# An adaLN transformer block: the order of ScalarE's first square roots, identity products on TensorE, and the place of the row modulation

## The reference, cut to what matters

```
mod = (silu(c) @ wmod).reshape(4, 6, 1, 256)
sa, ca, ga, sb, cb, gb = (mod[:, n] for n in range(6))
ga, gb = (2 * (g >= 0) - 1) * maximum(abs(g), 0.25)      # for both gates
h = layernorm(x) * (1 + ca) + sa                          # x is (4, 1024, 256)
x = x + ga * attention(h)                                 # 16 heads of 16
h = layernorm(x) * (1 + cb) + sb
x = x + gb * (mixture of 32 experts, 6 of them per token, and a shared expert)(h)
```

## Time and profile before

| | |
|---|---|
| time, median of 3 runs | 1390.08 us (1389.21 to 1391.02) |
| the profiled execution | 1387.17 us |
| its span | 1385.1 us |
| TensorE busy | 1329.3 us, 96% |
| VectorE busy | 1118.9 us, 81% |
| ScalarE busy | 737.3 us, 53% |
| GpSimd busy | 650.8 us, 47% |

### The profile page before, as it was taken

The page is one execution under the profiler, slowest core; times in us unless marked ns, Lnnn a source line. Parts: engine busy times, 40 slices in busy tenths (PEclk is TensorE's granted clock), DMA queues, the critical chain, the costliest instruction groups (busy, mean ns, idle before and its releaser), DMA issues.

```text
span 1385.1 us, 30718 instructions
## 1 busy us (share of the span) xinstructions
PE 1329.3 (96%) x8199; PEld 661.3 (48%) x8200; DVE 1118.9 (81%) x2809; ACT 737.3 (53%) x1127; POOL 650.8 (47%) x941
## 2 busy tenths in 40 slices
PE   6999999999999999999999999999999999999895
PEld 4562223323323223233232333577788888888542
DVE  6879999999999999999999983755566666666498
ACT  3551777767776777677776776123333333343100
POOL 1300123425745746557456467357655555555200
PEclk9996899999999999999999999999999999999998
DMA  6678655436356355463554437767666656665698
GB/s 208 225 232 199 136 159 104 93 78 151 67 139 149 97 116 113 120 166 64 130 145 148 116 112 236 229 195 230 219 201 200 204 176 186 178 176 177 254 340 328
DMA packets 264906, 235.31 MB, mean 170 GB/s; under 512 B 159286, under 2 KB 230470, under 8 KB 264684
## 3 DMA queue, kind: packets, MB, share of 16 engines
q1 hardware_dynamic: 237452, 159.23, 44.5%
q0 software_dynamic: 21872, 68.07, 13.7%
q10 hardware_dynamic: 5488, 6.82, 1.5%
HBM read 129.78 MB, written 104.22 MB: 169 GB/s over the span
## 4 chain that ended last, share of the span: by engine, by line
PE 70%; DVE 13%; DMA 4%; issue 2%; ACT 1%; POOL 1%; SPq 0%; DVEq 0%; ACTq 0%; POOLq 0%
PE psO L1274 15%; PE psE L1261 14%; PE ex_psGU L1787 12%; PE psM L1251 10%; DVE piece_max L1150 8%; PE ex_psY L1802 6%; PE ex_psX L1776 3%; PE psM L582 2%; DMA wide<-results 2%; PE ex_psA L1796 2%; PE co_psS L2056 2%; DMA results<-vals_inv,places 1%; ACT wide L1215 1%; PE late_psGU L2036 1%; PE late_psX L2047 1%
## 5 line engine op out<-in xcount | busy, mean ns | idle before, releaser
L1150 DVE TENSOR_REDUCE piece_max<-psM 128x1 f32<-128x512 f32 x1024 | 642.1, 681 | 19.4 <-PE psM L1251 15.8
L1215 ACT ACTIVATE wide<-psE 128x1024 f32<-128x1024 f32 x512 | 496.9, 1021 | 199.2 <-PE psE L1261 196.1
L1251 PE MATMUL psM<-wide 48*128 48x512 bf16 x1024 | 322.9, 394 | 9.3 <-DVE piece_max L1150 7.2
L1261 PE MATMUL psE<-wide 49*128 49x512 bf16 (+1 forms) x2048 | 328.9, 380 | 3.0 <-ACT wide L1215 2.8
L1868 POOL DMA_INDIRECT results<-vals_inv,places x223 | 213.9, 959 | 152.7 <-DVE vals_inv L1854 88.2
L1274 PE MATMUL psO<-wide 128*32 128x512 f32 x2048 | 273.6, 606 | 0.6 <-ACT wide L1215 0.6
L1251 PEld LDWEIGHTS psM<-wide 48*128 48x128 bf16 x1024 | 78.0, 93 | 334.0 <-DVE piece_max L1150 277.3
L1787 PE MATMUL ex_psGU<-wide,ex_xT 128*128 x892 | 231.1, 382 | 0.7 <-ACT ex_xT L1819 0.7
L1261 PEld LDWEIGHTS psE<-wide 49*128 49x128 bf16 (+1 forms) x2048 | 117.2, 95 | 94.2 <-ACT wide L1215 13.7
L1787 PEld LDWEIGHTS ex_psGU<-wide,ex_xT 128*128 128x128 f32 x892 | 152.1, 190 | 14.9 <-issue 2.7
L1819 ACT ACTIVATE ex_xT<-ex_psX 128x256 f32<-128x256 f32 x223 | 85.4, 383 | 123.3 <-PE ex_psX L1776 121.5
(11 more groups left out here) (285 smaller groups left out, 1248.1 us busy)
## 6 DMA issues: line engine op xcount, KB each, us to landing
wide<-qk_parts SPq DMA_DIRECT2D x384, 64.0 KB
wide<-results SPq DMA_DIRECT2D x16, 1536.0 KB, 9.4
rows<-lists SPq DMA_DIRECT2D x112, 160.0 KB
h2Ts<-lists SPq DMA_DIRECT2D x111, 160.0 KB
qk_parts<-parts SPq DMA_DIRECT2D x32, 384.0 KB, 2.9
xin<-in_x_dram SPq DMA_DIRECT2D x16, 512.0 KB, 4.1
wide<-in_guT_dram SPq DMA_DIRECT2D x3, 2560.0 KB, 13.6
lists<-pad_row SPq DMA_DIRECT2D x32, 160.0 KB
```

The source lines that it names most:

```text
L1150: v.tensor_reduce(piece_max[:, qh, (x * PAIRS + h) * KT // QH + qt, kh:kh + 1], bank_of("piece", PIECES * group + n), AX.X, ALU.max, negat ...
L1215: nc.scalar.activation(probs[:, step % 2, 2 * pair:2 * pair + 2], psE[:, pair], ACT.Exp, scale=HD ** -0.5).then_inc(exp_ok, 1)
L1251: nc.tensor.matmul(bank_of(*user), qa[g][rows, h, qt * P:(qt + 1) * P], ka[g][rows, h, kh * 512:(kh + 1) * 512], start=True, stop=True).th ...
L1261: mm = nc.tensor.matmul(psE[:, pair, x], k[g][part, pair, kt * P:(kt + 1) * P], q[g][part, pair, qh * 512:(qh + 1) * 512], start=(q is qa) ...
```

## The change

Three things. On ScalarE `modulate(0, k)` stands ahead of `deviation(1)`. On TensorE 12, 4 and 5 products of the identity with itself (`keep_clock`, 128 columns, into a part of `psV` that nobody reads) stand ahead of `modulation()`, behind it, and behind `turn(0)`. And the row modulation moves from chunk 1, where it came after the keys, into the last chunk, where there is no next chunk to turn or modulate: it takes the place of `turn` on TensorE and of `modulate` on ScalarE, with its result in `psT`. Its two loops are exchanged.

```
--- before.py
+++ after.py
@@ -156,7 +156,7 @@
     NARROW = 2 * D
     WIDE = 4 * D
     SHARE = 5
-    ROWS_AT = 1
+    WARM = (12, 4, 5)
     with ExitStack() as ctx:
         def sb(name, shape, dt):
             return ctx.enter_context(nc.sbuf_tensor(name, shape, dt))
@@ -441,15 +441,17 @@
             def rows_modulation():
                 act.wait_ge(rows_done, 1)
                 for n in range(4):
-                    nc.scalar.activation(mod_rows[row_of[n]], psV[row_of[n], 1, 0], ACT.Copy).then_inc(rows_ok, 1)
+                    nc.scalar.activation(mod_rows[row_of[n]], psT[row_of[n], 0, 0:D], ACT.Copy).then_inc(rows_ok, 1)
 
             def chunk(c):
                 first(c, 0)
                 second(c, 0)
                 first(c, 1)
-                for k in range(KC):
-                    if c + 1 < NCH:
+                if c + 1 < NCH:
+                    for k in range(KC):
                         modulate(c + 1, k)
+                else:
+                    rows_modulation()
                 second(c, 1)
                 if c + 2 < NCH:
                     deviation(c + 2)
@@ -457,16 +459,14 @@
                 first(c, 3)
                 second(c, 2)
                 second(c, 3)
-                if c == ROWS_AT:
-                    rows_modulation()
 
             act.dma_start(wmod_c[:], wmod[:, :, 0:NARROW]).then_inc(wmod_c_in, 16)
             act.wait_ge(c_in, 16)
             nc.scalar.activation(scT[:], cT[:], ACT.Silu).then_inc(silu, 1)
             deviation(0)
-            deviation(1)
             for k in range(KC):
                 modulate(0, k)
+            deviation(1)
             for c in range(NCH):
                 chunk(c)
 
@@ -480,6 +480,10 @@
                         mm = nc.tensor.transpose(psT[:, k, i * P:(i + 1) * P], xhat[:, c % 2, i, k * P:(k + 1) * P],
                                                  env.ident[:])
                     mm.then_inc(turned, 1)
+
+            def keep_clock(n):
+                for _ in range(n):
+                    nc.tensor.matmul(psV[:, 0, 0, 0:P], env.ident[:], env.ident[:], start=True, stop=True)
 
             def queries_keys(c, j):
                 if j == 0:
@@ -506,17 +510,15 @@
 
             def rows_modulation():
                 pe.wait_ge(wmod_r_in, 16)
-                pe.wait_ge(v_ok, 2 * ROWS_AT)
-                for n in range(4):
-                    for k in range(KC):
-                        last = nc.tensor.matmul(psV[row_of[n], 1, 0], scT[:, k], wmod_r[:, k, n * D:(n + 1) * D],
+                pe.wait_ge(modulated, KC * NCH)
+                for k in range(KC):
+                    for n in range(4):
+                        last = nc.tensor.matmul(psT[row_of[n], 0, 0:D], scT[:, k], wmod_r[:, k, n * D:(n + 1) * D],
                                                 start=(k == 0), stop=(k == KC - 1))
                 last.then_inc(rows_done, 1)
 
             def values(c):
                 for n in range(2):
-                    if c == ROWS_AT and n == 1:
-                        pe.wait_ge(rows_ok, 4)
                     wait(pe, v_ok, 2 * (c - 1) + n + 1)
                     for i in range(2):
                         for k in range(KC):
@@ -524,19 +526,22 @@
                                                   env.wqkv[:, 2, k, :], start=(k == 0), stop=(k == KC - 1))
                     mm.then_inc(v_done, 1)
 
+            pe.wait_ge(zero, 2)
+            keep_clock(WARM[0])
             modulation()
-            pe.wait_ge(zero, 2)
+            keep_clock(WARM[1])
             turn(0)
+            keep_clock(WARM[2])
             pe.wait_ge(chan_ok, 2)
             for c in range(NCH):
                 queries_keys(c, 0)
                 queries_keys(c, 1)
                 if c + 1 < NCH:
                     turn(c + 1)
+                else:
+                    rows_modulation()
                 queries_keys(c, 2)
                 queries_keys(c, 3)
-                if c == ROWS_AT:
-                    rows_modulation()
                 values(c)
```

## The result

The changed kernel takes 1394.73 us in the median of 11 runs (1391.37 to 1398.74), the kernel before 1390.08 in 11 runs on the same chip. The ratio is 1.0032, with a 95% interval of 1.0021 to 1.0043: 2.9 to 6.0 us slower. The forecast was 1392.6 in a range of 1388.0 to 1396.0.

The account below looks back on a forecast made before the run. VectorE was taken to set the pace in the projection phase's steady chunks, with a five-engine barrier behind it. GpSimd's late last arrival (+2.3) and a slow first attention product (+0.2) gave +2.5 us: 1392.6, range 1388.0 to 1396.0.

Parts of the forecast that it names:

- The front: Start of the projection phase: TensorE's first products at 13.5 rather than 16.54, VectorE's first split at 18.85, 1.94 us sooner.
- VectorE sets the pace: Steady chunks: normalisations 11.25 us apart set the time; TensorE by itself can gain no more than 0.8 us.
- My sum over VectorE: Projection phase: VectorE reaches its last normalisation 5.16 us sooner; with 0.6 of slack TensorE reaches the last chunk 5.76 sooner.
- The bearing of a failed clock: Start: products beginning at 15.5, two of them slow, still give the whole 1.94 us at VectorE's first split.
- rival B: Start: identity products stay slow and in the way, first products at 17.2, +5.9 us, 1396.0; chance 0.09.
- GpSimd's tail: Last chunk: GpSimd's row work loses its cover, lands at 113.0 less 0.4, so the last arrival is +2.3 us.
- my reduction by 0.4: GpSimd's row work in the last chunk: taken 0.4 us shorter than in chunk 1, from a range of nothing to 0.8.
- rival A: End of the projection phase: GpSimd's row work is hidden, phase ends with VectorE at -4.7 us, 1385.4; chance 0.09.
- Rival C: Attention phase: low clock reaches further, 1.5 to 2.5 us more, 1394.1 to 1395.1; chance 0.12, with a GpSimd DMA drain.
- the -4.7 that I had for the other engines: End of the projection phase: TensorE, VectorE and ScalarE finish 4.7 us sooner, from -5.76 and +1.07.

Follow-up runs that it names:

- e5: The changed kernel measured again without alteration, on another chip; ratio 1.0022 to the kernel before, boundary 113.38.
- e6: The changed kernel without the 21 identity products; ratio 1.0042 to the kernel before, boundary 114.11.
- e10: The changed kernel with GpSimd's row work behind the barrier and without the identity products; ratio 0.9967 to the kernel before, boundary 107.75.
- e9: The changed kernel with GpSimd's row work behind the barrier, measured a second time; ratio 0.9972 to the kernel before, boundary 106.42.
- e4: The changed kernel plus 36 identity products on TensorE behind the last values; ratio 1.0029. Its mark is VectorE's second transposed row of maxima.
- e3: The changed kernel with GpSimd's nine row operations, four DMAs and their wait moved behind the barrier; ratio 0.9977, median 1385.59 against 1389.2 us.
- e8: The changed kernel with only GpSimd's wait for the four DMA landings moved behind the barrier; ratio 1.0043 to the kernel before, boundary 113.33.

## Why the prediction was right, and where a size was off

**The front.** The numbers are right, and close: products at 13.39 for 13.5, VectorE's first split at 18.94 for 18.85, its normalisations at 27.60, then 11.26 us apart until 83.89, which is 5.03 us sooner than before (forecast 5.16). TensorE 5.62 sooner at the last chunk (5.76).

The reason that I gave for them, that in the steady chunks "VectorE sets the pace", holds for one profile only, the changed kernel's first. There TensorE has 67.55 us between chunk 1 and the last chunk, 0.4 more than its own 67.17. In every other profile, e5 of the same kernel too, TensorE runs through these chunks without a wait for VectorE, 11.20 us a chunk; VectorE takes 11.26, and TensorE's lag of 0.8 us is not used up within eight chunks. So what comes sooner at the last chunk is what TensorE's own chunk 1 begins sooner (3.7 us here, 3.3 in e5) and the 2.3 us less in chunk 1. My sum over VectorE gave 3.26 for the first (TensorE's 0.6 included) and 2.50 for the second. That the two ways come within 0.3 us of each other is luck, and this part of the forecast owes its size to it.

**The bearing of a failed clock.** The prediction says that "products that start at 15.5, two of them slow, still give all of it". That is right for VectorE's first split and wrong for the end of the phase. In e6 the split does not wait, and yet the 0.75 us that TensorE begins chunk 1 later are 0.73 at the boundary; in e10 against e9 it is 1.33 for 1.33. It was no idle question. The granted clock stayed up in the changed kernel's first profile only. In e9, which is one of seven later profiles with identity products, all with a turn of 1.97 us, it was down before the turn:

```profile
8.74 2.05 PE L490 MATMUL psV<-ident 128*128 128x128 f32 x8
11.12 1.97 PE L484 MATMUL psT<-ident,xhat 128*128 128x128 f32 x8 [0.32 <-DVE xhat L339]
12.88 2.17 PE L490 MATMUL psV<-ident 128*128 128x128 f32 x10
14.89 3.60 PE L499 MATMUL psQK<-hT,wqkv 128*128 128x512 f32 x8
```

The five behind the turn then end at 15.0 and not at 13.3, where the chunk is ready at 13.9: for a slow clock they stand in the way by 1 us. In e9 the clock is back for the wide products (3.60 us for eight passes), so rival B (products at 17.2) did not occur, and VectorE's split is at 18.67 even so.

**GpSimd's tail.** The step on which the sign rested, and it was right: copies at 97.77 for 97.7, GpSimd at 99.52 for 99.43. Its sizes were off in three places that nearly cancel. The nine operations and the issues took 11.4 us from the first to the last issue's start, the same 11.44 as in chunk 1, so my reduction by 0.4 was wrong: L262 did come down (1.07 and 1.10), but L260 took 1.21 and L263 1.07 once each, beside VectorE, and the first issue took 0.79 again, with VectorE idle. The landings took 1.6 to 1.8 and not 2.1; the last was at 112.5. And the barrier opened 0.8 after it, not the 0.4 that it takes behind SyncE's last issue. Together +2.6 at the boundary for +2.3, and with VectorE's first maximum 0.2 later +2.8.

On rival A: the Trainium skill (SBUF — State Buffer, Who interferes with whom) names an exclusive lock between GpSimd and VectorE. The trace agrees that the same shape has a long and a short form, 1.07 and 0.72 for L263. It disproves rival A, in which the lock had stretched them all: the last four operations, nearly all of them with VectorE done (105.5), still take 3.84 us from start to end (104.90 to 108.74).

**The rest.** The measured 4.65 us is 1.9 above the 2.8 of the boundary and the first maximum. The lower end of the interval, 2.9, comes close to it, and the second measurement gives 3.3; where the rest comes from stays open. Part of the excess in the profile is plain: the profiled execution is the slowest of the 11, and 3.5 us of it come around one dip of the clock (granted 0.74 within 400 to 410), of which the profile before has none. VectorE's transposed maxima are 3.1 us later than before ahead of it (399.92 for 396.83) and 6.6 behind it.

```profile
400.00:410.00 10.00, 10.00 (x65) 2.51 (x61) 7.95 (x20) 6.20 (x7) 2.33 (x8) 0.74 0.46 93
```

The profile of e3, a faster kernel, has low stretches there as well (0.99 granted over 400 to 860, as in the changed kernel; 1.00 before). Whether the changed kernel has more of them is open; e4 was made to catch a link to the standstill and shows none. Rival C, 1.5 to 2.5 us more behind the boundary, is not seen: the mark of e4 lies 42.4 to 43.8 us behind the boundary with an idle standstill, and 42.7 to 43.4 without one.

e3 gives what rival A had promised in another way: the tail is not hidden where it stands, but it is when the same work stands behind the barrier. Most of the -4.7 that I had for the other engines then shows: -3.2 and -3.9 us in two measurements (e3 and e9), with boundaries 3.8 and 4.3 sooner.

## What to carry to other kernels

Work that is moved to a free slot of one engine takes its followers on the other engines along; here the slot on TensorE and ScalarE was free, but thirteen microseconds of GpSimd work lost their cover and stood alone ahead of a barrier. Before moving something toward a barrier, list everything behind it on every engine up to the last wait, and ask whether that needs to be on this side: moving it across made the change a gain. And before you say that two edits help only together, look whether their profiles had the same start: here 1.2 and 0.7 us of the difference was the clock of the first products in single profiles, and with it taken out the two parts add. When two engines run within 1% of each other per chunk (11.20 and 11.26 us here), a slack read at one of them doesn't show that the other has any.

## What had not been expected of the hardware

Removing a wait for small GpSimd DMAs ahead of a barrier brought 0.4 us of the 1.1 that the wait seemed to take (e8). TensorE's granted clock fell at the start in seven of eight profiles although products ran on: in e9 the 8 passes from 8.74 are already slow (granted clock 0.50 from 8 to 9), right behind 40 passes without a pause longer than 0.63 us. And on one chip every kernel took 8% longer (1498.73 against 1389.2 us for the same program); the projection phase there is as long as elsewhere (boundary 113.38 for 113.31), while the window of 860 to 1000 us has TensorE busy for 113 of 140 us and not 133 (e5 against the kernel before). I have no cause for it.
